# Expert row tiles ordered by the arrival of their first rows, and most of the result groups combined inside the expert stages

## What is computed

```python
x = x + _L0_attn_a_ref(_layernorm(x), Wqvk, Wo)      # causal attention over tokens
x = x + _L0_ffn_ref(_layernorm(x), gate_w, gate_b, w1, b1, w2, b2)
x = x + _L0_attn_b_ref(_layernorm(x), ...)           # attention over the 16 heads of each token
x = x + _L0_ffn_ref(_layernorm(x), ...)

def _L0_ffn_ref(x, gate_w, gate_b, w1, b1, w2, b2):  # 24 experts, top 2 of them, 128 -> 512 -> 128
    gate_scores = jnp.einsum('bsd,de->bse', x, gate_w) + gate_b
    topk_val, topk_idx = lax.top_k(gate_scores, TOP_K)
    sparse_gates = jax.nn.softmax(topk_val, axis=-1)
    ...
    h = jax.nn.gelu(jnp.einsum('bsd,edf->besf', x, w1) + b1[None, :, None, :], approximate=False)
    y = jnp.einsum('besf,efd->besd', h, w2) + b2[None, :, None, :]
    out = jnp.einsum('bse,besd->bsd', combine, y)
    return out + x
```

## Time and profile before

| | |
|---|---|
| median of 3 runs | 1154.83 us |
| the runs | 1166.44, 1154.83, 1153.0 us |
| span of the profiled execution | 1188.8 us |
| PE busy, share of the span | 1006.9 us, 85% |
| DVE | 757.1 us, 64% |
| ACT | 698.1 us, 59% |
| POOL | 738.2 us, 62% |

### The profile page before, as it was taken

How to read it: one execution, slowest core, us unless ns; L and a number is a source line. 1 busy time by engine, 2 the same in 40 slices (tenths; PEclk the granted TensorE clock), 3 DMA queues, 4 the chain that set the end, 5 groups by cost and what they waited for, 6 DMA issues and landing times.

```text
span 1188.8 us, 28731 instructions
## 1 busy us (share of the span) xinstructions
PE 1006.9 (85%) x9491; PEld 779.4 (66%) x9494; DVE 757.1 (64%) x2104; ACT 698.1 (59%) x2115; POOL 738.2 (62%) x1075
## 2 busy tenths in 40 slices
PE   4999998898989981899999889888898817999990
PEld 2555555554555541899999377767776617999990
DVE  3688878777777933344444388899999742444444
ACT  3578776776767641455556366676757424555650
POOL 8545465657657226455566588789998563665661
PEclk8699999999999965899999989999989957999995
DMA  9999980000000002566675699996000015676757
GB/s 339 389 388 391 349 293 8 14 8 20 9 13 13 11 17 71 153 197 190 192 198 163 238 379 389 391 391 165 12 19 19 21 43 166 197 206 197 203 160 212
DMA packets 121847, 203.12 MB, mean 171 GB/s; under 512 B 13280, under 2 KB 67224, under 8 KB 121574
## 3 DMA queue, kind: packets, MB, share of 16 engines
q1 hardware_dynamic: 107750, 182.25, 46.9%
q0 software_dynamic: 9728, 16.95, 4.2%
q10 hardware_dynamic: 4224, 2.10, 0.6%
HBM read 76.72 MB, written 127.65 MB: 172 GB/s over the span
## 4 chain that ended last, share of the span: by engine, by line
PE 35%; POOL 22%; issue 18%; DVE 15%; ACT 5%; DMA 2%; another core or an unknown queue 1%; POOLq 1%; ACTq 0%; SPq 0%; DVEq 0%
POOL rows_out L815 14%; PE bank L1413 6%; PE bank L1021 5%; PE bank L1374 5%; PE bank L1334 3%; PE bank L1355 3%; POOL SETTLE L814 3%; DVE QK L1123 2%; DVE NMP L1595 2%; POOL rows_in L671 2%; PE bank L1392 2%; PE bank L1329 2%; DMA PT<-rows_out 2%; POOL PT L958 1%; PE bank L555 1%
## 5 line engine op out<-in xcount | busy, mean ns | idle before, releaser
L840 ACT ACTIVATE QT<-bank,B 128x128 f32<-128x128 f32 x704 | 201.2, 368 | 184.2 <-PE bank L863 100.0
L1537 ACT ACTIVATE PT<-bank 128x512 f32<-128x512 f32 x320 | 188.3, 604 | 89.0 <-PE bank L1355 88.4
L815 POOL DMA_INDIRECT rows_out<-Y,XI x176 | 174.7, 992 | 91.3 <-POOL SETTLE L814 84.3
L863 PE MATMUL bank<-XIT,PT 128*128 128x128 f32 x1408 | 192.3, 281 | 3.1 <-DVE XIT L916 1.8
L874 PE MATMUL bank<-W,QT 128*128 x1408 | 187.9, 277 | 1.3 <-ACT QT L840 1.3
L863 PEld LDWEIGHTS bank<-XIT,PT 128*128 128x128 f32 x1408 | 174.5, 195 | 5.8 <-DVE XIT L916 2.7
L874 PEld LDWEIGHTS bank<-W,QT 128*128 128x128 f32 x1408 | 172.8, 193 | 1.6 <-issue 1.6
L958 POOL TENSOR_TENSOR PT<-PT 128x512 f32<-128x512 f32 x128 | 157.5, 1262 | 23.6 <-ACT PT L1064 22.4
L671 POOL DMA_INDIRECT rows_in<-XG,POS x128 | 126.4, 988 | 49.0 <-issue 35.0
L1374 PE MATMUL bank<-KT,QT 48*128 48x384 bf16 (+3 forms) x512 | 125.3, 316 | 11.1 <-DVE NMP L1591 7.5
L921 DVE TENSOR_TENSOR YB<-bank,B2R 128x128 f32<-128x128 f32 x176 | 51.3, 292 | 122.7 <-PE bank L874 75.2
(11 more groups left out here) (213 smaller groups left out, 1985.3 us busy)
## 6 DMA issues: line engine op xcount, KB each, us to landing
rows_in<-XI SPq DMA_DIRECT2D x32, 3120.0 KB, 28.9
PT<-in_w_dram SPq DMA_DIRECT2D x176, 256.0 KB
XI<-rows_in SPq DMA_DIRECT2D x176, 65.0 KB
W<-in_w2pack_dram SPq DMA_DIRECT2D x4, 1536.0 KB
PT<-rows_out SPq DMA_DIRECT2D x24, 256.0 KB, 6.1
rows_in<-XI SPq DMA_DIRECT2D x2, 1560.0 KB
rows_out<-Y,XI POOLq DMA_INDIRECT x176
X<-in_h_dram SPq DMA_DIRECT2D x8, 256.0 KB, 5.2
```

Of the source, the lines that this page charges most:

```text
L815: pool.indirect_dma_start(out=rows_out, out_offset=bass.IndirectOffsetOnAxis(ap=XI_I[:, u, D + 1:D + 2], axis=0), in_=Y[:, u % 4, :], in_o ...
L840: a = act.activation(HT[:, u % 2, c, :], psH[u % 2][:, c * P:(c + 1) * P], ACT.Gelu, bias=B1[:, bass.ds(e * FC + c, 1)])
L863: mm = pe.matmul(psH[u % 2][:, c * P:(c + 1) * P], W1[:, u, c * P:(c + 1) * P], XIT[:, u % 2, :], start=True, stop=True)
L1537: act.activation(PT[:, m % PT_SLOTS, :], psB[m % 2][:, :], ACT.Exp, scale=float(D) ** -0.5).then_inc(exp_done, 1)
```

## The change

The row tiles take another order. RUNS keeps the counts after each group, instead of RUN alone, and a tile is placed by the group in which its first row was written and only then by expert (8 x 24 cells). So all rows of group g lie in the first 8(g+1)+23 tiles (`last_tile_of`), and its results are complete in rows_out well before the stage ends, but for the last group. The tables grow to cells. Their larger part (`head_tables`, groups 0 to 6, 192 cells wide at most) runs on DVE while the last group is still on its way; the rest (`expert_tables`) follows the last group.

Groups 0 to 6 are then fetched by SP inside the loop over row tiles (at j = 38, 46, ... 86), combined by DVE inside it (at j = 36, 44, ... 84; SP runs ahead of DVE), and in stage 1 also sent (from j = 45). Only group 7 is fetched, combined and sent after the stage. In stage 0 the statistics and the power of groups 0 and 1 also move into the stage. POOL no longer combines in attention b, the 48 filler matmuls go, PE waits for the last result only ahead of its first sum, and all zero fills are issued behind the last fetch. The fetched results lie in buffers that the weights don't use.

```diff
-SPIN_FETCH, SPIN_TURNED, SPIN_QUERIES, SPIN_EXPS = 48, 2, 2, 18
+SPIN_TURNED, SPIN_QUERIES, SPIN_EXPS = 2, 2, 18
...
+def last_tile_of(g):
+    return (2 * (g + 1) * GT * P + NE * (P - 1)) // P - 1
+def fetch_at(g):
+    return last_tile_of(g) + STEP
+def combine_at(g):
+    return last_tile_of(g) + 6
+def send_at(g):
+    return fetch_at(g) + 7
...
+        def tile_counts(dve, link, q0, q1):
+            rows = slice(0, ROW_TILES)
+            counts = TK.rearrange("p (q e) -> p q e", e=NE)[:, q0:q1]
+            whole = TI[:, q0 * NE:q1 * NE]
+            link(dve.tensor_tensor(counts, RUNS[rows, q0:q1, :],
+                                   RUNS[rows, 0:1, :].broadcast_to([ROW_TILES, q1 - q0, NE]), ALU.subtract))
+            link(dve.tensor_scalar(whole, TK[:, q0 * NE:q1 * NE], float(P - 1), None, ALU.add))
+            link(dve.tensor_scalar(whole, whole, 7, None, ALU.arith_shift_right))
+            link(dve.tensor_copy(TK[:, q0 * NE:q1 * NE], whole))
+        def cell_places(dve, link, c0, c1):
...
+        def passed_cells(dve, link, c0, c1, total):
+            steps = TSUM[:, 0:2 * (c1 - c0)].rearrange("p (a c) -> p a c", a=2)
+            link(dve.tensor_tensor(TDV[:, c0:c1], TV[:, c0 + 1:c1 + 1], TV[:, c0:c1], ALU.subtract))
+            dve.scalar_tensor_tensor(steps[:, 0], TEND[:, c0:c1], IOTA_J[:, :], DE[0:ROW_TILES, c0:c1], ALU.is_le, ALU.mult)
+            link(dve.scalar_tensor_tensor(steps[:, 1], TEND[:, c0:c1], IOTA_J[:, :], TDV[:, c0:c1], ALU.is_le, ALU.mult))
+            link(dve.tensor_reduce(total, steps, AX.X, ALU.add))
+        def head_tables(dve, ph):
+            link = linker(dve, e_link, E_LINKS * ph)
+            dve.wait_ge(r_link, R_LINKS * (GROUPS * (ph + 1) - 1))
+            tile_counts(dve, link, 0, GROUPS)
+            cells = CELLS - NE
+            link(dve.tensor_tensor(TN[:, 0:cells], TK[:, NE:NE + cells], TK[:, 0:cells], ALU.subtract))
+            link(dve.tensor_tensor_scan(TEND[:, 0:cells], ones_over(cells), TN[:, 0:cells], 0.0, ALU.mult, ALU.add))
+            link(dve.tensor_copy(TN[:, cells - 1:cells], TEND[:, cells - 1:cells]))
+            link(dve.memset(TV[:, CELLS:CELLS + 1], float(DUMMY)))
+            cell_places(dve, link, 0, cells)
+            passed_cells(dve, link, 0, HEAD, ERB[:, :])
+            link(dve.tensor_tensor(ERB[:, 1:2], ERB[:, 1:2], TV[:, 0:1], ALU.add))
+            link(dve.scalar_tensor_tensor(ERB[:, 1:2], IOTA_J[:, :], float(P), ERB[:, 1:2], ALU.mult, ALU.add))
...
         def fetch(eng, ph, g, k):
-            buffers = len(f_yc[ph])
-            before = ph * GROUPS + max(g + 1 - buffers, 0)
-            if before > 0:
-                eng.wait_ge(f_done, before)
-            eng.dma_start(YC[:, 4 - buffers + g % buffers, k, :, :],
-                          rows_out_v[:, k, g * GT:(g + 1) * GT, :]).then_inc(f_yc[ph][g % buffers], 16)
+            if 4 <= g < GROUPS - 1:
+                eng.wait_ge(f_done, ph * GROUPS + g - 3)
+            eng.dma_start(arrived(g)[:, k, :, :],
+                          rows_out_v[:, k, g * GT:(g + 1) * GT, :]).then_inc(f_yc[g], 16)
...
@@ experts_sp @@
+            def body(j, u):
+                load(j, u)
+                for g in range(GROUPS - 1):
+                    if j == fetch_at(g):
+                        fetch(sp, ph, g, 0)
+                        fetch(sp, ph, g, 1)
+                    if ph == 1 and j == send_at(g):
+                        send_group(g)
...
@@ experts_pool, body(j, u) @@
+                for g in range(2):
+                    if ph == 0 and j == combine_at(g) + 6:
+                        group_power(pool, GROUPS + g, g)
...
@@ experts_dve, body(j, u) @@
+                for g in range(GROUPS - 1):
+                    if j == combine_at(g):
+                        if g == 0:
+                            dve.wait_ge(r_xadd, GROUPS * (ph + 1))
+                        combine(dve, ph, g)
+                    if ph == 0 and g < 2 and j == combine_at(g) + 2:
+                        dve.wait_ge(f_done, g + 1)
+                        for i in range(6):
+                            group_stats(dve, GROUPS + g, GT * g, g, i)
+                        add_eps(dve, GROUPS + g, MEAN[:, g * GT:(g + 1) * GT, :], f_var, f_eps)
...
+            combine(dve, ph, GROUPS - 1)
...
@@ attb_pool, attb_pe, attb_dve @@
-                if s % GT == 0 and 2 <= g + 2 < GROUPS:
-                    combine(pool, 0, g + 2, g % 2)
...
-            group_power(pool, GROUPS, 0)
+            pool.wait_ge(f_done, GROUPS - 1)
...
+                    if T == 0:
+                        pe.wait_ge(f_y, ROW_TILES)
...
+                if T == 4 * GROUPS + 5:
+                    head_tables(dve, 1)
...
-            pe.wait_ge(f_y, ROW_TILES)
-            spin(pe, psF, SPIN_FETCH)
             attb_pe(pe)
...
@@ block.vector, slot(n, u, k) @@
+                    if g == GROUPS - 2 and j == 43:
+                        dve.wait_ge(scoresB_done, STEPS * UNITS)
+                        head_tables(dve, 0)
```

More of the change, by code:

```diff
@@ L141, in hybrid_layer, with scratch @@
         EXP1 = sb("EXP1", [P, GT])
[L142 to L143 removed]
+        RUNS = sb("RUNS", [P, GROUPS + 1, NE])
         POS = sb("POS", [P, 2, GT, 2], I32)
[L146 to L151 removed]
+        spent_kt = KT[0:ROW_TILES, :, :, :, :].rearrange("p r g t c -> p (r g t c)").bitcast(F32)
+        def scratch(at, n):
+            return spent_kt[:, at:at + n]
+        TK = scratch(0, CELLS + NE)
+        TI = spent_kt.bitcast(I32)[:, CELLS + NE:2 * (CELLS + NE)]
+        TN, TEND = scratch(2 * (CELLS + NE), CELLS), scratch(3 * CELLS + 2 * NE, CELLS)
+        TV, TDV = scratch(4 * CELLS + 2 * NE, CELLS + 1), scratch(5 * CELLS + 3 * NE, CELLS)
+        TSUM = scratch(6 * CELLS + 3 * NE, 2 * CELLS)
+        DE = sb("DE", [P, CELLS])
+        ERB = sb("ERB", [ROW_TILES, 2])
         ERF = sb("ERF", [ROW_TILES, 2])
@@ L170, in hybrid_layer, with arrived @@
         Y = sb("Y", [P, 4, D])
-        YC = in_keys.rearrange("p (a k t d) -> p a k t d", a=4, k=2, t=GT)
+        ahead_of_last = weights[:, 8 * FF:16 * FF].rearrange("p (a k t d) -> p a k t d", a=4, k=2, t=GT)
+        of_last = weights[:, 4 * FF:6 * FF].rearrange("p (k t d) -> p k t d", k=2, t=GT)
+        def arrived(g):
+            return of_last if g == GROUPS - 1 else ahead_of_last[:, g % 4]
         f_w_in = sem("f_w_in")
@@ L226, in hybrid_layer @@
         f_ys = [sem(f"f_ys{i}") for i in range(STEP)]
-        f_yc = [[sem(f"f_yc{ph}{i}") for i in range(2 + 2 * ph)] for ph in range(2)]
+        f_yc = [sem(f"f_yc{g}") for g in range(GROUPS)]
         f_ysum = sem("f_ysum")
@@ L618, in route_rows @@
             wait(dve, r_link, R_LINKS * n + 12 + min(i, 3))
+            before, after = (RUNS[:, n % GROUPS + more, :] for more in range(2))
             if i == 0:
@@ L626, in route_rows @@
             if i == 1:
-                dve.tensor_tensor(RUN[:, :], RUN[:, :], psG[:, 2 * GT * NE:(2 * GT + 1) * NE], ALU.add)
+                dve.tensor_tensor(after, before, psG[:, 2 * GT * NE:(2 * GT + 1) * NE], ALU.add)
                 dve.tensor_tensor(O1H[0][:, :, :], O1H[0][:, :, :], CAND, ALU.mult)
@@ L696, in expert_tables @@
+            cell_places(dve, link, cells, CELLS)
+            passed_cells(dve, link, HEAD, CELLS, ERF[:, :])
+            dve.tensor_tensor(ERF[:, :], ERF[:, :], ERB[:, :], ALU.add).then_inc(e_flat, 1)
             dve.wait_ge(e_turned, ph + 1)
@@ L782, in load @@
                     load_weights(j, u)
-            over_rows(load, read_ahead(sp, f"sp_number{ph}", (EJ, NE - 1), (RJ, DUMMY)))
             def send_group(g):
@@ L788, in send_group @@
                 sp.dma_start(out_v[:, g * GT:(g + 1) * GT, :], X[:, g * GT:(g + 1) * GT, :]).then_inc(out_sent, 16)
+            def body(j, u):
[6 more added lines that the diff above has]
+                        send_group(g)
+            over_rows(body, read_ahead(sp, f"sp_number{ph}", (EJ, NE - 1), (RJ, DUMMY)))
             for i in range(STEP):
                 sp.wait_ge(f_ys[i], 16 * (ROW_TILES // STEP) * (ph + 1))
-            for g in range(GROUPS):
-                fetch(sp, ph, g, 0)
-                if ph == 0:
-                    fetch(sp, ph, g, 1)
-                    if 3 <= g <= GROUPS // 2 + 2:
-                        sp.wait_ge(f_refill, 2)
-                        empty_rows(sp, 1, g - 3)
-                if ph == 1 and g >= SEND_LAG:
-                    send_group(g - SEND_LAG)
+            fetch(sp, ph, GROUPS - 1, 0)
+            if ph == 0:
+                fetch(sp, ph, GROUPS - 1, 1)
+                sp.wait_ge(f_refill, 2)
+                for c in range(GROUPS // 2):
+                    empty_rows(sp, 1, c)
             if ph == 1:
-                for g in range(GROUPS - SEND_LAG, GROUPS):
-                    send_group(g)
+                for g in range(GROUPS):
+                    if send_at(g) >= ROW_TILES:
+                        send_group(g)
         def experts_pool(pool, ph):
@@ L847, in experts_act @@
```

(11 more changed lines are left out.)

76 lines of the change are left out of this document (31 added, 45 removed).

## The result

| | before | after |
|---|---|---|
| median of 20 runs each | 1154.91 us | 1148.96 us |
| lowest and highest | 1151.56, 1166.44 | 1141.43, 1155.40 |
| ratio after/before, 95% interval | | 0.9935, 0.9914 to 0.9956 |
| span of the first profiled execution | 1188.8 us | 1147.9 us |

What follows compares the result with a forecast made beforehand. PE was taken to bound the expert stages, DVE to be nearest its bound in attention b, and chains the seams. Terms 0.2 + 3.4 + 2.0 + 16.3 + 5 - 11.9 - 2.5 - 15.0 = -2.5 on 1154.8 gave 1152 us, range 1134 to 1175.

Steps and rivals of the forecast that it cites:

- Behind stage 1, -15.0: After stage 1: two DMAs fetched instead of sixteen and one group combined, so the span ends 15.0 us earlier.
- Behind stage 0, -11.9: Seam after stage 0: POOL's first products start once XI is refilled, at 661.0 instead of 672.86, 11.9 us earlier.
- Start, +3.6 (0.2 and 3.4): Before stage 0: wider constants cost POOL 0.2 us; `head_tables` delays the last batch's addition and the scatters by 3.4.
- Ahead of stage 1, +2.0: Before stage 1: logits 1.6 us later, two more table operations 0.4; all counts because the tables' way is the later.
- Inside the stages, +16.3: Expert stages: 14 combinings on DVE each stall PE 1.0 us (14.0), plus statistics of two groups in stage 0 (2.3).
- DMA inside the stages, +5: Expert stages: fetches and sends on the weights' queue cost a quarter of a us each, 5 us, bounds 0 to 35.
- fetches late: Rival: in the stages fetches land 2.5 us after DVE's turn or hold weights back as much; +30, 1182 us, chance 0.12.
- the same stall of 1.0 us mostly covers that: Expert stages: weights of tiles 39 and 40 wait behind the fetch, mostly hidden by PE's 1.0 us stall at a combining.
- Attention b, -2.5: Attention b: POOL loses six combinings, so DVE's small operations stand less behind POOL; 2.5 us shorter, bounds 0 to 15.1.
- POOL is the bound: Rival: POOL bounds attention b, so 12.6 us more come back; 1140 us, chance 0.10.
- POOL's lock (rival): In the stages POOL's SETTLE waits for both additions, making a store 1.4 us late; 6 us more, 1158 us, chance 0.10.
- The insertions cost PE nothing (rival): In the stages PE's queue has more slack than 0.44 us, so 16.3 us less; 1136 us, chance 0.13.

Runs made afterwards that it cites:

- spin30: The changed kernel with 30 instead of 18 filler matmuls behind the fourth transposition of attention b; 1142.97 us, ratio 0.9875 to the kernel before.
- head: The changed kernel with `head_tables` of stage 0 moved behind the last group's statistics; 1147.25 us, ratio 0.9890 to the kernel before.
- before_again: The kernel before, unchanged, profiled a second time; attention b took 255.8 us.
- tinyfetch: The kernel gap with fetches of groups 0 to 6 bringing 8 of 128 partitions, so their results don't reach X; 1136.39 us in its one run.
- gap: The changed kernel with a combining's two additions in two row tiles, beside PE's down matmuls, and statistics spread over three; 1147.84 us, ratio 0.9916 to before.
- after_early: The changed kernel with only the weights loaded two tiles earlier; 1142.62 us, ratio 0.9872 to the kernel before.
- early: The kernel best1 with each tile's weights loaded two tiles earlier, as in after_early; 1132.94 us, ratio 0.9774 to the kernel before.
- after_again: The changed kernel, unchanged, profiled and timed a second time; 1147.24 us, ratio 0.9922 to the kernel before.
- split: The kernel gap with a fetch's two DMAs behind two tiles, combining one and send two tiles later; 1142.96 us, ratio 0.9878 to the kernel before.
- best1: The changed kernel with the edits of gap, split, head and spin30 together; 1139.11 us, ratio 0.9828 to the kernel before.

## Why the prediction was right and where it was not

The time was right to 3 us (1152 forecast, 1149), and the terms behind the two stages and at the start were right by their mechanism. That the rest came out as well is luck: the stages grew by 6.3 us less than forecast and the way ahead of stage 1 by 2.1 less, while attention b came out 5.9 us longer than forecast, and these nearly cancel. The 2% that the prediction took for the least that can be told was too wide a limit: with 20 runs each the interval of the 0.65% ends clear of no change. Means of after's segments against those of before give the terms (the second and third profile of before for the start and the way ahead of stage 1, all three elsewhere); the plain after is after twice, with spin30 and head where they leave a segment as it is.

**Behind stage 1, -15.0:** measured -14.5 (25.47 to 11.00). **Behind stage 0, -11.9:** -11.4 (20.86 to 9.42). Both by the way forecast, from last store to fetch and POOL's refill.

**Start, +3.6 (0.2 and 3.4):** +4.0 (450.1 to 454.1), of which head gave back 2.8.

**Ahead of stage 1, +2.0:** -0.1 (62.85 to 62.7). The delay at the logits is there, 1.6 us, but the segment isn't longer. The step that failed is "the last scatter is issued at 979.21 and the rows are loaded at 983.92 ... so the tables' way is the later one". In that execution SP issued the weights late, from 981.29 to 983.67, and the rows right behind them. In all 13 others the weights were issued 2 to 3 us ahead of the last scatter, so the scatters' way is the later one and the tables' operations don't count. The timeline of before_again has it:

```profile
941.55 1.93 SPq L762 DMA_DIRECT2D PT<-in_w_dram  x4
...
944.43 0.96 POOL L671 DMA_INDIRECT rows_in<-XG,POS  x1 [0.30 <-issue]
...
947.74 2.40 SPq L767 DMA_DIRECT2D XI<-rows_in  x5
```

The 4.7 us don't tell the two apart: the step is 3.3 and 3.5 us in the two other profiles of before, but 4.5 to 4.6 in six traces of the change, with the weights early. The 1.6 us at the logits are made up ahead of them. In ten of the eleven traces of the change PE ends the last logits' matmuls 31.4 to 31.6 us behind the last reduction (32.8 in tinyfetch), in those of before 32.9 to 34.0; the last scatter follows at 48.6 to 49.0 us (50.0), before 49.1 to 50.2. Why that part is shorter isn't settled.

**Inside the stages, +16.3:** right in place and mechanism (XIT late, PE waits, gap removes it), too large in size. By gap it is 3.8 and 1.0 us, by after_early and early 5.7 and 1.8: 5 to 8 us. A combining that showed on PE cost 0.3 to 0.7 us, and not all did: in after_again PE has 9 and 4 waits for XIT, 4.1 and 1.2 us in total, where the prediction had 1.0 us at each of 14. The term was 1.42 less the 0.44 us of slack of one tile; the queue has more than that tile shows, by how much at each place wasn't measured.

**DMA inside the stages, +5:** 11.2 by tinyfetch (3.4 and 7.8), 7.2 by the weights' lead alone. The fetches landed in time: in after one combining of the 14 inside the stages waited, for 0.4 us, and the median landing was 4.5 us where the earlier trace rows have 6.1. So the mechanism of the rival "fetches late" fell, and the sentence "the same stall of 1.0 us mostly covers that" failed: the weights behind the fetch were late by more than the stall. The growth of the two stages together, 21.3 forecast, was 15.0 (169.5 to 176.5 and 168.9 to 176.9). An overestimate of 8 to 11 us and an underestimate of 2 to 6 cancelled in part.

**Attention b, -2.5:** its seven traces with attention b unedited have a mean of 257.0 us (252.4 to 261.0), before's three 253.6. That it got shorter isn't borne out. The reason given, that DVE's small operations would no longer stand behind POOL's combinings, failed: operations on 4 columns that took over 0.5 us number 10, 11 and 10 in before and 13, 6, 7, 9, 11, 14 and 12 after, 10.3 on average in both. In before only 6 of the 31 lie beside a combining of POOL and 25 beside its products, after all 72 beside products. The traces with 6 and 7 of them are the ones of 252 and 253 us. Of the 3.4 us, 0.8 are the one profile of before with the whole clock at the 11th reduction, and three of the seven have a step of 11.0 to 13.7 us behind the 17th. Whether the 3.4 us are the change's, through longer idle stretches of PE and the clock behind them, or scatter, stays open. The rival "POOL is the bound" fell: 19 us of POOL's work went and nothing came back.

**POOL's lock (rival):** inside the stages both additions took 0.69 us, and POOL's SETTLE beside them 0.38 to 0.56 instead of 0.18, in 12 places of after (576.54 to 577.10, say, over a first addition that ended at 577.05). It waited for the rest of one addition and never for both, so the lock costs 0.2 to 0.4 us there, not 1.4. The blocked operation of the earlier trace rows, by which the prediction judged this, has one tensor as its input, not two; the additions of the seam are the case with two. It was dear in one place, beside the products (1.75 and 1.64 us).

**The insertions cost PE nothing (rival):** not in after; true of gap, where PE has no wait for XIT left.

The sum of the segments' means is 4.0 + 7.0 - 11.4 + 3.4 - 0.1 + 8.0 - 14.5 = -3.6 us, without attention b -7.0; the runs gave -6.0 and, in the comparison of after_again, -10.2.

## What to carry to other kernels

Work moved into a stage with a busy bottleneck is nearly free if each piece stands behind the operation that the bottleneck waits for and beside its longest step, and costs if it stands ahead of it; ask the same of a transfer: put it behind loads that have lead to spare, and free a ring's place when its reader is done (the up matmuls) rather than when a later step is (the store). Here the weights' lead alone took the gain from 0.65% to 1.3%; with the additions moved, the fetches split, `head_tables` moved and 30 fillers it came to 2.3%. Before a term is drawn from a single wait of a single execution, look whether the next execution has it.

## What the hardware showed that wasn't expected

The granted clock fell to its lower level behind an idle stretch of PE of only 1.65 us, in the middle of a stage in which PE is 88% busy, and one step grew from 9.4 to 13.7 us (head, split, early). In three other traces with the same idle stretch at the same place it didn't (after, best1, after_early). At the 11th reduction it fell behind an idle stretch of 1.09 us in 13 traces of 14, and the step there took 2.4 us or more longer than in the one where it held. So the idle stretch alone doesn't decide it. Such falls, with what DVE's small operations lose behind POOL's products (1.1 to 1.2 us for 0.17), go with a scatter of attention b over 251 to 261 us for one and the same work.
